# Second expert layer with W2 as the moving operand: 128 slots by fp32r parts, 40 slots in fp32 in two column tiles

## What is computed

```
x = x + gat(layernorm(x), adj, W, a1, a2)
x = x + ffn(layernorm(x), Wr, br, W1, b1, W2, b2)

# ffn: E = 8 experts, C = 1354 // 8 = 169 places each, positions from 1 on, so 168 can be taken
probs = softmax(x @ Wr + br); gate = max(probs); idx = argmax(probs)
mask = one_hot(idx); pos = cumsum(mask) * mask; mask = mask * (pos < C)
dispatch = combine = gate * one_hot(expert) * one_hot(place)
expert_in = einsum('nd,nec->ecd', x, dispatch)          # gathered rows, scaled by the gate
h  = relu(einsum('ecd,edf->ecf', expert_in, W1) + b1)   # first layer
eo = einsum('ecf,efd->ecd', h, W2) + b2                 # second layer
out = einsum('ecd,nec->nd', eo, combine)                # back to the rows, by the gate
```

## Time and profile before

| | us |
|---|---|
| median of 3 runs (266.55 to 268.67) | 267.65 |
| the profiled execution, its own time | 269.95 |
| its span, first to last instruction | 267.0 |
| PE busy, of 267.0 | 252.2 |
| DVE busy | 152.4 |
| ACT busy | 113.1 |
| POOL busy | 80.4 |

### The profile page before, as it was taken

One profiled execution on the slowest core, in us unless ns is written; L12 is line 12 of the kernel. 1 busy time (PEld: TensorE's weight loads), 2 busy tenths in 40 slices (PEclk: granted clock), 3 DMA queues, 4 the chain that ended last, 5 costly groups with the idle time before them and its releaser, 6 DMA issues.

```text
span 267.0 us, 4737 instructions
## 1 busy us (share of the span) xinstructions
PE 252.2 (94%) x1721; PEld 225.1 (84%) x1721; DVE 152.4 (57%) x394; ACT 113.1 (42%) x236; POOL 80.4 (30%) x113
## 2 busy tenths in 40 slices
PE   6699989999999999999999999997999999999990
PEld 2399989988887877877878899897999999999980
DVE  4888678996978797776733566725023322332140
ACT  2637786855575557466443222311312323314110
POOL 4334890000343242021022060155504153222022
PEclk9999999999999999999999999999999999999997
DMA  6990000330588887212121112127995878873001
GB/s 202 358 307 28 1 5 0 106 104 19 190 233 239 286 281 251 84 69 77 39 81 39 41 60 75 45 73 218 352 296 185 255 247 291 223 231 136 8 7 43
DMA packets 18201, 38.62 MB, mean 145 GB/s; under 512 B 2698, under 2 KB 3018, under 8 KB 18180
## 3 DMA queue, kind: packets, MB, share of 16 engines
q1 hardware_dynamic: 15188, 32.34, 37.1%
q0 software_dynamic: 2176, 4.80, 6.3%
q10 hardware_dynamic: 816, 1.21, 1.3%
HBM read 31.10 MB, written 8.31 MB: 148 GB/s over the span
## 4 chain that ended last, share of the span: by engine, by line
PE 79%; DMA 6%; DVE 4%; POOL 3%; issue 3%; ACT 2%; another core or an unknown queue 1%; POOLq 1%; ACTq 0%; DVEq 0%
PE bank L1370 29%; PE bank L1612 23%; PE bank L1308 6%; PE bank L1356 5%; DMA x_rows<-x_all 3%; PE bank L1695 2%; PE bank L1385 2%; DMA w_raw<-in_L_gnn_W_dram 2%; PE bank L1290 2%; PE bank L1397 2%; PE bank L1408 1%; DMA wide<-x_rows,src 1%; PE bank L1604 1%; PE bank L1336 1%
## 5 line engine op out<-in xcount | busy, mean ns | idle before, releaser
L1370 PE MATMUL bank<-h_hi,pt_lo 128*128 128x512 f32 (+1 forms) x110 | 45.9, 417 | 0.0
L1370 PE MATMUL bank<-h_lo,pt_hi 128*128 128x512 f32 (+1 forms) x110 | 43.6, 396 | 0.0
L1370 PE MATMUL bank<-h_hi,pt_hi 128*128 128x512 f32 (+1 forms) x110 | 43.4, 394 | 0.0
L406 POOL TENSOR_TENSOR x_all<-x_all,w_raw 128x512 f32<-128x512 f32 x10 | 18.1, 1807 | 65.2 <-ACT w_raw L584 65.2
L1612 PE MATMUL bank<-prob,w 128*128 128x168 f32 x224 | 33.2, 306 | 0.0
L1612 PEld LDWEIGHTS bank<-prob,w 128*128 128x128 f32 x224 | 32.3, 190 | 0.0
L1612 PE MATMUL bank<-adj_s,w 128*128 128x168 f32 x208 | 31.0, 306 | 0.3 <-ACT adj_s L724 0.3
L1612 PEld LDWEIGHTS bank<-adj_s,w 128*128 128x128 f32 x208 | 29.8, 190 | 0.7 <-issue 0.7
L724 ACT ACTIVATE adj_s<-bank,b_cols 128x168 f32<-128x168 f32 x28 | 9.7, 397 | 36.9 <-PE bank L1612 36.9
L1370 PEld LDWEIGHTS bank<-h_hi,pt_hi 128*128 128x128 f32 (+1 forms) x110 | 20.7, 188 | 4.9
L1370 PEld LDWEIGHTS bank<-h_hi,pt_lo 128*128 128x128 f32 (+1 forms) x110 | 20.7, 189 | 3.8
(11 more groups left out here) (185 smaller groups left out, 476.0 us busy)
## 6 DMA issues: line engine op xcount, KB each, us to landing
w<-in_L_ffn_W_dram SPq DMA_DIRECT2D x16, 1024.0 KB, 6.1
adj_s<-in_adj_dram SPq DMA_DIRECT2D x10, 677.0 KB, 5.6
x_rows<-x_all SPq DMA_DIRECT2D x10, 257.0 KB, 3.6
out_dram<-x_all SPq DMA_DIRECT2D x10, 256.0 KB
x_all<-in_x_dram SPq DMA_DIRECT2D x9, 256.0 KB, 5.7
w_raw<-in_L_gnn_W_dram ACTq DMA_DIRECT2D x4, 256.0 KB, 5.7
adj_s<-in_adj_dram SPq DMA_DIRECT2D x1, 391.4 KB
x_all<-x_rows,src POOLq DMA_INDIRECT x10, 6.3
```

Source lines behind the costliest of these rows:

```text
L406: pool.tensor_tensor(x_all[0:R, t, 0:D], x_all[0:R, t, 0:D], relu_s[0:R, :], ALU.add).then_inc(s_x1, 1)
L1370: ins = pe.matmul(o_ps[par][0:R, :], p[0:K, par, k, 0:R], h[0:K, k, :], start=(k == 0 and n == 0), stop=(k == NT - 1 and n == 2))
```

## The change

For experts 1 to 7 the second layer is turned round. W2 moves and the hidden values are stationary, so the result has slots on the partitions at once, and out_turn falls away; b2 is then a row and not a column. The 168 slots are cut into 128 and 40 (S = (P, CAP - P)) everywhere: gathers, scatters, preparation, transposes, routing sums.
- `wide_part` (PE): 128 slots, W2 in 4 pieces of 128x512, fp32r parts, 3 x 4 = 12 matmuls of 512 columns into one bank. ACT makes the high parts of W2 (`w2_high`, two halves of 1024 columns) and of the hidden values (a second relu of 128 columns beside each of 168); DVE makes the low parts (`w2_low`, two halves of 1024; `hid_low`, two of 256).
- `narrow_part` (PE): 40 slots, fp32, two column tiles side by side, tile i for the output columns i x 256 to i x 256 + 255: 8 matmuls of 256 columns.
- b2 comes by SP as a row broadcast to 128 partitions (`load_b2`, 256 KB), three buffers; DVE adds gate x b2 to the gathered rows (`out_bias`), 128x512 and 40x512, ahead of the products.
- Order: PE wide 0, narrow 0, narrow 1, wide 1 (last expert: wide 0, narrow 0, wide 1, narrow 1). The loops are written out; `load_w2` from expert 3 on waits for the results of e - 2.
- Expert 0 keeps its form but for the cut.

The core of the diff:

```diff
+    S = (P, CAP - P)
...
+            def load_b2(e):
+                i = (e - 1) % 3
+                if e > 3:
+                    sp.wait_ge(s_vb, 2 * (e - 3))
+                sp.dma_start(b2_b[i], b2[e, :].partition_broadcast(P)).then_inc(s_b2[i], 16)
...
             sp.wait_ge(s_x1g[2], 32)
-            sweep(sp, load_expert, 0, 0, E, start=2)
+            sp.wait_ge(s_prob, NT)
+            sp.wait_ge(s_pt[2], NT)
+            for e in range(2, E):
+                load_w1(e)
+                if e == 2:
+                    load_b2(1)
+                load_b2(e)
+                load_w2(e)
...
+            def w2_high(e):
+                par = e % 2
+                act.wait_ge(s_w2[par], landed(e, par))
+                if e >= 3:
+                    act.wait_ge(s_y, 2 * e - 2)
+                for q in range(2):
+                    act.activation(w2_hi[par][:, 2 * q:2 * q + 2, :], w2_s[:, par, 2 * q:2 * q + 2, :], ACT.Copy
+                                   ).then_inc(s_w2hi, 1)
...
+            gx_copy(0)
             act.wait_ge(s_bc, 1)
...
+            w2_high(1)
+            hid_relu_first()
+            eo_bias_low()
+            gx_copy(1)
+            for e in range(1, E):
+                hid_relu(e)
+                if e + 1 < E:
+                    gx_copy(e + 1)
+                    w2_high(e + 1)
...
+            def out_bias(e):
+                i = (e - 1) % 3
+                dve.wait_ge(s_b2[i], 16 * ((e - 1) // 3 + 1))
                 for j in range(2):
+                    v = x1_g[e][0:S[j], j, 0:D]
                     dve.wait_ge(s_xg, e * 2 + j + 1)
+                    dve.scalar_tensor_tensor(v, b2_b[i][0:S[j], :], gate_s[0:S[j], j, e:e + 1], v, ALU.mult, ALU.add
+                                             ).then_inc(s_vb, 1)
...
             hid_relu_first()
-            for e in range(E):
+            w2_low(1)
+            prepare(1)
+            eo_bias_high()
+            out_bias(1)
+            for e in range(1, E):
+                if e == 1:
+                    final_first()
+                else:
+                    final(e - 1)
                 if e + 1 < E:
                     prepare(e + 1)
...
+                hid_low(e)
+                if e + 1 < E:
+                    w2_low(e + 1)
+                    out_bias(e + 1)
+            final(E - 1)
...
+            def wide_part(e, q):
+                par = e % 2
+                pe.wait_ge(s_w2lo, 2 * (e - 1) + q + 1)
+                pe.wait_ge(s_hidlo, 2 * (e - 1) + q + 1)
+                for c in range(2 * q, 2 * q + 2):
+                    for n, (v, w) in enumerate(((hid_lo, w2_hi), (hid_hi, w2_lo), (hid_hi, w2_hi))):
+                        ins = pe.matmul(ya_ps[par][:, :], v[par][:, c, :], w[par][:, c, :],
+                                        start=(c == 0 and n == 0), stop=(c == KC - 1 and n == 2))
+                if q:
+                    ins.then_inc(s_y, 1)
+
+            def narrow_part(e, q):
+                par = e % 2
+                pe.wait_ge(s_hidv, 2 * (e - 1) + q + 1)
+                for c in range(2 * q, 2 * q + 2):
+                    for i in range(2):
+                        ins = pe.matmul(yb_ps[par][64 * i:64 * i + S[1], 0:H0], hid[par][:, c, P:CAP],
+                                        w2_s[:, par, c, i * H0:(i + 1) * H0], start=(c == 0), stop=(c == KC - 1),
+                                        tile_position=(0, 64 * i))
+                if q:
+                    ins.then_inc(s_y, 1)
```

More of the change, by code:

```diff
@@ L243, in adj_in, with parts @@
             eng.wait_ge(s_adj[t % 3], 16 * (t // 3 + 1))
-        def after_halves(eng, sem_, e, lag):
-            if not isinstance(e, int) or e >= lag:
-                eng.wait_ge(sem_, e * 2 - 2 * (lag - 1))
+        def parts(e):
+            return (0, 1) if e in (0, E - 1) else (1, 0)
         def hold(eng, sem_, value):
@@ L254, in hold @@
             eng.sem_inc(s_held, 1)
[L256 to L266, removed]
         block = ctx.enter_context(nc.Block())
@@ L708, in gx_copy @@
+                    if e == 0 and j == 0:
                         ins.then_inc(s_gx0, 1)
                 ins.then_inc(s_gxt, 1)
[L711 to L726 removed]
@@ L1596, in _, with in_turn @@
             late_first(NT - 1, 2, KC)
-            def in_turn(e, par):
+            def in_turn(e):
                 pe.wait_ge(s_xg, e * 2 + 2)
-                after(pe, s_gxt, e, 1)
+                pe.wait_ge(s_gxt, e)
                 for c in range(KC):
@@ L1611, in layer, with first_layer @@
+            def first_layer(e):
+                par = e % 2
+                pe.wait_ge(s_w1[par], landed(e, par))
+                pe.wait_ge(s_gxt, e + 1)
+                if e >= 2:
+                    pe.wait_ge(s_hidv, 2 * e - 2)
+                for f in range(KC):
                     for c in range(KC):
-                        ins = pe.matmul(ps[f // 2][:, (f % 2) * CAP:(f % 2 + 1) * CAP],
-                                        w[:, c, f * P:(f + 1) * P], v[:, c, :], start=(c == 0), stop=(c == KC - 1))
+                        ins = pe.matmul(hid_ps[f // 2][:, (f % 2) * CAP:(f % 2 + 1) * CAP],
+                                        w1_s[:, par, c, f * P:(f + 1) * P], gx_t[par][:, c, :],
+                                        start=(c == 0), stop=(c == KC - 1))
@@ L1721 @@
+            second_layer_first()
+            in_turn(1)
+            out_turn_first()
+            for e in range(1, E):
+                first_layer(e)
+                if e + 1 < E:
+                    in_turn(e + 1)
+                second_layer(e)
 _INS = ["x", "adj", "L0_gnn_W", "L0_gnn_a1", "L0_gnn_a2", "L0_ffn_Wr", "L0_ffn_br", "L0_ffn_W1",
```

399 lines of the change are left out of this document (177 added, 222 removed).

## The result

The changed kernel takes 279.89 us (277.47 to 282.81), the kernel before 267.7 beside it: 1.043 times as long, 95% interval 1.033 to 1.052. Forecast were 269.2 us and at most 276. The profiled execution took 277.47 us, span 275.7.

What follows compares the result with a forecast made beforehand. PE was taken to bound the kernel (79% of what ended last). Wait and gain cancelled to -0.2 us (263.3 for 263.5); with 1.7 for the clock, +1.5 on the median 267.65 gave 269.2 us, range 265.2 to 276.

Steps and rivals of the forecast that it cites:

- the price of turn in: Eight transposes of gathered rows per expert, four of 128 columns and four of 40: 0.65 us, between 0.58 and 0.87.
- b2 late, DVE's order, PE's wait: Expert 1's b2 lands at 190.3, DVE's preparation of expert 2 queues behind it, PE waits 4.5 us before in_turn(2).
- The first rival: Start of the experts: b2 not late, landing before 187.5, or the clock stays up; 264.2 us, chance 0.15.
- the second: Rival on the load queues: each b2 broadcast costs 4.3 us; 275.5 us in the middle, chance 0.22.
- The clock: PE's granted clock falls behind the wait before in_turn(2), costing between 1 and 3 us, taken as 1.7.
- Narrow part: Second layer's 40 slots, 8 fp32 matmuls in two column tiles side by side: 1.74 + 0.28 = 2.02 us.
- The third rival: Narrow part: the two column tiles don't run side by side, 1.74 us more in each of seven experts, 281; chance 0.07.
- The 0.28 us for going in and out of the tiles: Narrow part: array drain when changing tiling mode, read from the logit strips, added to 1.74 us.
- Wide part: Second layer's 128 slots, 12 fp32r matmuls of 512 columns, priced like the attention's: 2.80 us.
- DVE's and ACT's chain: Expert periods: DVE's work done at T + 14.5, wanted at T + 14.6; period 10.2 us, PE alone 10.05.
- the fourth rival: Expert periods: DVE's and ACT's work sets the period at 10.9 us, total 272.7 us; chance 0.12.
- Last expert: Kernel's end: from F, its first layer's end, to the last scatter's issue F + 7.9, saving 2.6 us.

Runs made afterwards that it cites:

- early b2: Changed kernel with the b2 loads of experts 1 to 3 issued ahead of SP's wait for expert 2's gathers: 276.42 us, ratio 1.028.
- the grouping: Changed kernel with turn in of experts 1 to 7 doing the four 128-row transposes first, then the four of 40 rows: 276.33 us, ratio 1.023.
- the all-row version: Changed kernel with each 40-slot transpose in turn in of experts 1 to 7 made a plain matmul over all 128 rows: 277.33 us, ratio 1.029.
- the two single cures: Changed kernel with either b2 loaded early (ratio 1.028) or prepare(2) and hid_low(1) moved ahead of out_bias(1) and final_first on DVE (ratio 1.029).
- DVE's order alone: Changed kernel with prepare(2) and hid_low(1) ahead of out_bias(1) and final_first on DVE, b2 loads left late: 276.42 us, ratio 1.029.
- the last three kernels: Changed kernel with early b2, new DVE order and grouped turn in; then narrow part first; then w2_low(2) behind prepare(3): 267.64, 266.08, 264.71 us.
- the kernel with both cures: Changed kernel with b2 of experts 1 to 3 loaded early and DVE's order around expert 1 changed: 271.74 us, ratio 1.0055.

## Why the prediction was wrong

The step that failed is the price of turn in: 0.65 us in the sum, 1.61 measured. The forecast had end points in times of the trace; here is each beside what the profile shows.

- **b2 late, DVE's order, PE's wait**: right. The issue of W1 and the landing of b2 were taken at 182.96 and 190.3, they are 183.25 and 191.06; the wait is 4.8 us for 4.5. The first rival (b2 not late) and the second (4.3 us per broadcast) are out: it landed 0.9 us behind W1 (taken: 1.2), and of the later ones PE waited for none. But the mechanism was told half. The early b2 shows that `final_first`, which `prepare(2)` now also stands behind, would have held PE by itself.
- **The clock**: right that it falls, 2.5 us for 1.7, within the 1 to 3. The 4.0 us without work that the prediction read from the trace's end were no lower bound: the early b2 shows a fall behind 1.9 us.
- **Narrow part**: 1.86 us for 2.02, tiles side by side. The third rival is out by the run without tiles. The 0.28 us for going in and out of the tiles is not borne out as a price of them: 1.86 is 0.12 over the 1.74 of the estimate, and the wide half behind costs the same without tiles.
- **Wide part**: 2 x 1.59 = 3.18 us for 2.80, 0.38 too low. In the earlier trace rows 12 such matmuls stand in one piece among their like; here they are cut in two, and each half pays about 0.2 us on entry, behind 40 rows or 40 columns.
- **Turn in**: "I take 0.65, between 0.58 and 0.87" is the step that failed. It is 1.61. I counted columns only, and 0.87 was no bound: no row of before had transposes of two row counts in turns. That the turns cost it is shown by the cut alone (1.62), the grouping (0.81) and the all-row version (no standstill). The Trainium skill's rule that I cited for the column tiles (TensorEngine Tiling (Array Packing), Key Properties: a change of tiling mode drains the engine) would fit here too, if 40 rows alone put the array into another mode; no tile is named in the code, and no run shows a mode. The trace shows the weight loads standing still for 0.17 to 0.20 us at a change and 0.13 us per change, and I had asked that rule only where the diff says `tile_position`.
- **DVE's and ACT's chain**: it did not set the period. PE waits for DVE once in all the experts. The 0.15 us of allowance was not used, and the fourth rival is out.
- **Last expert**: from F = 264.87 to the last scatter's issue, 272.65, 7.8 us for 7.9.

The sum: the second layer of expert 1 ends at 204.18 for 199.8. Of these 4.4 us the later end of the wait has 0.7, turn in at half clock 2.06 (2.71 for 0.65), the layer 1.65. Five periods of 11.22 (from 204.18 to 260.28) for 10.2 are 5.1 more. Together 9.5 us, of which turn in has 0.96 in each of the five periods and 2.06 in the first turn, 6.9 us. The forecast had 1.7 of the 9.5 as its term for the clock. Of the other 7.8, turn in at full clock has 6 x 0.96 = 5.8. The last scatter's issue so ends at 272.65, 9.1 us later than before, and the two profiled executions lie 7.5 apart (277.47 and 269.95), since 1.6 us less lie behind and around that point. The medians lie 12.2 apart, since the profiled execution of the kernel before is 2.3 above its median and that of the changed kernel 2.4 below. The other executions of the changed kernel have a mean clock of 0.970 to 0.976, the profiled one 0.982; that a longer fall makes the difference fits the run with 28 idle matmuls, but no profile of such an execution was taken.

The experiments bear the sum out by parts. Wait, clock and order are worth 1.043 - 1.0055, 3.7%, 10 us. Grouping is worth 1.7% more, 4.5 us of the 6.4 expected, with a new wait of 1.2 taking part of it. With these costs mended, the idea of the change itself is 1.1 to 1.3% faster than before.

## What to carry to other kernels

Where a diff cuts rows into unequal parts, look at what rows each matmul and transpose uses, and in which order: sort by row count. Here every change between 128 and 40 rows stopped the weight loads; other counts were not tried. Where an in-order engine gets a new wait, list all that stands behind it and what each would wait for in its turn; here the two single cures gained 1.5 and 1.4%, both together 3.7%. A wait on PE is to be priced with the clock that falls behind it, here half as much again.

## What the runs showed of the hardware that was not expected

- A transpose of 40 rows between ones of 128 costs some 0.13 us per change, on PEld as a standstill of 0.17 to 0.20 us. 40 stationary columns with all rows cost nothing of the kind: the dispatch (8 pairs of 128 and 40 columns in turns) takes 1.34 us in both kernels.
- PE's granted clock fell to 1.2 GHz around waits of 1.9, 2.06, 3.6, 4.5, 4.8, 6.6 and 8.1 us, in seven profiles, and 3.4 us (DVE's order alone) to 6.8 us (b2 early) of the work behind them ran at it, estimated from the mean clocks of stretches. Around waits of 1.7, 1.2 and 0.9 us among the experts (the last three kernels) it stayed at 2.4 GHz.
- It also falls where nothing was changed, in some executions only: in the profile of the grouped kernel it reads 0.50 from 14 to 18 us, behind an idle 1.74 us at 12 us, and the first turn in starts 3.9 us later than in the ungrouped one (169.16 for 165.22); the kernel with both cures had the same. The kernel before idles as long there, 1.73 us up to 11.2 us, and its clock stays at 1.00 in its profile: the length of the wait alone does not decide. In those of the cut alone and of all rows it is 0.87 and 0.84 from 150 to 160 us. Much of a kernel's scatter of 3 to 5 us may be that; it was not tested.
- A 256 KB broadcast of one row behind 1 MB in the same queue landed 7.0 to 10.2 us after its issue, in the seven profiles of kernels that load it so. A forecast that hangs on such a landing carries that spread of some 3 us.
- A group of fp32r matmuls of 512 columns pays about 0.2 us on entry behind transposes of 40 rows or matmuls of 40 stationary columns, column tiles or not (1.59 us for six), and nothing that shows directly behind an fp32 layer of full size (1.38 us for six); why was not settled.
